# Letting four gathers go at once, and turning two engines' loops at different units of a group

## The chip, the cores and the metric

The kernel runs on one core of a Trainium2 chip. The metric is the device time of one execution in microseconds (us). Three executions of the kernel before took 2305.17, 2313.61 and 2311.89 us; the median is 2311.89. The execution that the profiler recorded took 2306.23 us.

## The reference

x is 64 sequences of 32 tokens with 512 channels. Four additions follow each other; the third is where the time goes.

```
x = x + einsum('bct,bcd->bdt', x, W0[cond])              # one of 16 mixing matrices per sequence
x = x + (x @ base.T + bias + lora(x, id))                # a linear layer with one of 32 adapters
x = x + attention(x)                                     # below
x = x + einsum('bct,bcd->bdt', x, W3[cond])

# attention, D = 128, 32 query heads, 8 key heads
q, k, v = x @ Wq.T, x @ Wk.T, x @ Wv.T                   # q and k: RMS norm, then rotary positions
kc = k_cache[block_table]                                # 16 pages of 32 positions per sequence
vc = v_cache[block_table]
scores = q @ concat(kc, k).T / sqrt(D)                   # cached positions >= seqlen are masked
o = softmax(scores) @ concat(vc, v)
out = o @ Wo.T                                           # 4096 -> 512
```

All arithmetic is fp32; many products are made as three products of rounded high parts and low remainders (high x high, high x low, low x high).

## The kernel before

Four sequences (32 tokens each) make a group of 128 rows; there are NT = 16 groups and B = 64 sequences ("batches"). After the first two layers and the projections (up to about 700 us of the trace) comes the attention. Its unit of work is one key head of one sequence with its four query heads: UG = 32 units a group, 512 in all. The instruction streams of the five engines are written by hand and meet only in semaphores. Each engine has a function `step(g, u)` with what it does in unit u of group g:

- **TensorE** computes the scores two units ahead (`score(n + 2)`, six matmuls), turns the normalised scores of this unit (`turn_p`, four transposes), makes a few matmuls of the output projection of an earlier group (`out_proj`), and the values product of the unit before (`values`, eight matmul records). At the end of each sequence come the transposes and products of the sequence's own keys (`turn_own`, and 16 small matmuls at L1290).
- **VectorE** makes the low part of the keys three units ahead (`split_k`, L999), the masked maximum two units ahead (`masked_max`, L1014), and the normalisation one unit ahead (`inverse`, `normalise`, L1020 to L1026). In some units come the low part of q (L1005, u a multiple of 4), the next mask (L991, u % 8 == 5), the low half of a finished sequence's heads (`heads_low`, L1031, after the units in `HEADS_AT`) and, in the unit `RESIDUAL`, the addition of the projected rows to the residual (L1037).
- **ScalarE** rounds keys four units ahead (`split_k`, L730), takes the exponentials one unit ahead (L744), and copies the turned scores out of PSUM (L790).
- **SyncE** loads, for each sequence, q, its own k, 16 pages of cached keys of 128 KB (L378) and its own v; it stores the heads, and loads and stores the residual rows. Its `group` function is not touched; at k == 3 it waits for `s_x2y` (the residual addition) before it stores.
- **GpSimd** gathers the cached values: four indirect DMAs of 0.5 MB a sequence (L551) by a column of row numbers each, which it first copies out of `idx_all` (L548). The gathers of sequence b go out in the four units from u = 10 + 8k on. The first waits until the products of the sequence two before are done (`s_po`), the other three each wait for TensorE's transposes of the unit before (`s_ta`).

The output projection of one group is 48 matmuls of 512 columns into one PSUM bank, `yP`. `WO_AT` says how many of them each unit of the next group holds, `WO_FROM` where they begin: from unit 4 to unit 31, one or two a unit. The first waits for the low halves of the first 16 heads and for the residual addition of the sum before (`s_x2y`), the 25th for the low halves of the others; the 24th and the last are noted (`s_woh`, `s_wo`).

Groups 1 to 14 are a hardware loop (`Fori(1, NT - 1)`) on every engine, and groups 0 and 15 are written out on either side. On TensorE (L1346), ScalarE (L821) and VectorE (L1088) the loop turns between unit 31 and unit 0, on GpSimd between units 23 and 24.

Of the kernel before, what the change touches and what calls it, by code (L numbers as in the profile page):

```python
# [36 lines left out]
BT = P // C  # L37
NT = B // BT
# [5 lines left out]
UG = BT * HK  # L44
# [6 lines left out]
H2 = HQ // 2  # L51

WO_AT = {u: 1 if u in (7, 8, 15, 16, 23, 24, 30, 31) else 2 for u in range(4, UG)}
WO_FROM, at = {}, 0
# [4 lines left out]
HEADS_AT = {2: (1, 3, 0), 5: (1, 0, 1), 6: (1, 1, 1), 8: (1, 2, 1), 10: (1, 3, 1), 18: (0, 0, 0), 21: (0, 1, 0), 26: (0, 2, 0)}  # L59
RESIDUAL = UG - 1  # L60
WO_SPLIT = 8
# [18 lines left out]
def build(nc, x, cond_row, id_row, bt_row, idx_pages, seq_tok, seq_all, w0, w3, wb, bias,  # L80
# [3 lines left out]
    with ctx:  # L84
# [133 lines left out]
        idx_all = sb("idx_all", [P, (B + 1) * 4], I32)  # L218
        idx = [sb(f"idx{i}", [P, 4], I32) for i in range(4)]
# [302 lines left out]
        def _(pool):  # L522
# [21 lines left out]
            for j in range(4):  # L544
                pool.wait_ge(s_x2st[j], 16 * (NT // 4))
            def next_idx(b, k, m):

                nc.gpsimd.tensor_copy(idx[k][:, m:m + 1], idx_all[:, bass.ds(b * 4 + m, 1)]).then_inc(s_idx, 1)  # L548

# [5 lines left out]
            pool.wait_ge(s_idx0, 1)  # L555
            for b in range(3):
                for m in range(4):
                    next_idx(b, b, m)
            pool.wait_ge(s_idx, 8)
            for m in range(4):  # L560
# [16 lines left out]
            def step(g, u):  # L577
                fixed = isinstance(g, int)
                k, m = (u - 10) // HK, (u - 10) % HK
                if m < 4 and not (fixed and not 2 <= g * BT + k + 2 < B):  # L580
                    b = g * BT + (k + 2)
                    if m == 0:
                        pool.wait_ge(s_idx, b * 4 + 4)
                        pool.wait_ge(s_po, g * BT + (k + 1))
                    else:
                        pool.wait_ge(s_ta, g * UG + u)
                    next_idx(b + 1, (k + 3) % 4, m)
                    gather_v((k + 2) % 4, k % 2, m)
# [265 lines left out]
        def _(dve):  # L854
# [190 lines left out]
            def step(g, u):  # L1045
# [13 lines left out]
                if u - 1 in HEADS_AT:  # L1059
                    back, b, half = HEADS_AT[u - 1]  # L1060
                    if not (fixed and g < back):
                        heads_low(g - back, b, half, HI_COUNT[b, half])
                if u == RESIDUAL and not (fixed and g == 0):
                    residual(g - 1)

# [15 lines left out]
            for u in range(UG):  # L1081
                if u == 4:
                    for j in range(2):
                        dve.wait_ge(s_qst[j], 16 * QKB * NT // 2)
                step(0, u)
                if 0 <= u - WO_SPLIT < H2:
                    split_wo(0, u - WO_SPLIT, wo_lo, wo_raw)
            with dve.Fori(1, NT - 1) as g:  # L1088
                for u in range(UG):
                    step(g, u)  # L1090
            for u in range(UG):
                step(NT - 1, u)
            for u in list(HEADS_AT)[:5]:
                heads_low(NT - 1, *HEADS_AT[u][1:], HI_COUNT[HEADS_AT[u][1:]])
# [36 lines left out]
        def _(pe):  # L1131
# [186 lines left out]
            def step(g, u):  # L1318
# [4 lines left out]
                turn_p(g, u)  # L1323
                if u in WO_AT and not (fixed and g == 0):
                    out_proj(g - 1, WO_FROM[u], WO_AT[u])
                if u > 0:
                    values(g, u - 1)
                elif not (fixed and n == 0):
                    values(g - 1, UG - 1)
# [14 lines left out]
            for u in range(UG):  # L1344
                step(0, u)
            with pe.Fori(1, NT - 1) as g:  # L1346
                for u in range(UG):
                    step(g, u)
            for u in range(UG):
                step(NT - 1, u)  # L1350
            values(NT - 1, UG - 1)
            out_proj(NT - 1, 0, 3 * H2)

# [78 lines left out]
```

## Time and profile before

| | |
|---|---|
| three executions | 2305.17, 2311.89, 2313.61 us |
| profiled execution | 2306.23 us |
| span from the first to the last instruction | 2304.4 us |
| busy: TensorE matmul, VectorE, ScalarE, GpSimd | 2231.9, 1754.5, 1598.8, 598.2 us |
| granted TensorE clock, mean | 0.996 of full |

A busy TensorE is not one at its peak, since its matmuls are pipelined and their ends are modelled; the time between the starts of the same operation in neighbouring units tells more. The records of an engine's sequencer (register arithmetic, branches) carry a q behind the engine's name and are not counted as busy. A loop leaves three kinds of them on its own line: one MOVE, and for each pass a FUSED_REGOPS at its beginning and a COMPARE_BRANCH at its end. An idle time in brackets stands before the instruction of its line, with what the profile takes to have ended it; "issue" is idle time in which the engine waited for nothing that the profile shows.

### The profile page before, as it was taken

How to read it: one execution, taken by the hardware profiler on the slowest of the kernel's cores; microseconds unless marked ns; L12 is line 12 of the kernel's file. 1: busy time of each engine (PE TensorE's matmuls, PEld its weight loads, DVE VectorE, ACT ScalarE, POOL GpSimd, SP SyncE). 2: the span in 40 equal slices, each digit the busy share in tenths (PEclk: the TensorE clock that was granted, in tenths of full speed). 3: DMA queues.
4: the chain of work that ended last, by engine and by line, in shares of the span. 5: the costliest groups of instructions: out<-in, count | busy, mean ns of one | idle time of the engine just before them, and what ended most of it. 6: DMA issues, size and time to landing. Idle time of an engine off the chain costs nothing.

```text
span 2304.4 us, 57131 instructions
## 1 busy us (share of the span) xinstructions
PE 2231.9 (97%) x15424; PEld 2001.3 (87%) x15424; DVE 1754.5 (76%) x5602; ACT 1598.8 (69%) x4413; POOL 598.2 (26%) x907
## 2 busy tenths in 40 slices
PE   7999999999999899999999999999999999998999
PEld 6787888888888899999999999999999999997777
DVE  3434777777778998988888888898898898995332
ACT  4423666666667988888888888888888788884221
POOL 1003444444443322222222222222222222220000
PEclk9999999999999999999999999999999999999999
DMA  5335333333337887877887877887887877864332
GB/s 170 95 114 165 102 101 102 100 101 118 101 92 251 249 255 249 260 250 249 260 252 246 258 251 244 256 257 241 256 255 246 259 254 252 256 223 179 137 123 96
DMA packets 348202, 456.58 MB, mean 198 GB/s; under 512 B 34682, under 2 KB 281018, under 8 KB 343870
## 3 DMA queue, kind: packets, MB, share of 16 engines
q1 hardware_dynamic: 308430, 315.83, 44.5%
q0 software_dynamic: 36864, 134.23, 17.4%
q10 hardware_dynamic: 2672, 4.31, 0.5%
q14 instruction: 202, 1.65, 0.3%
q8 instruction: 34, 0.56, 0.1%
HBM read 374.54 MB, written 79.69 MB: 197 GB/s over the span
## 4 chain that ended last, share of the span: by engine, by line
PE 80%; DVE 9%; issue 7%; ACT 2%; DMA 1%; ACTq 0%; DVEq 0%; SPq 0%
PE oP L1280 14%; PE S L1247 13%; PE S L1204 12%; PE oP L1204 11%; PE S L1298 8%; PE bank L1134 7%; PE bank L1311 6%; DVE k_lo L999 3%; PE oP L1134 3%; PE oP L1162 2%; DVE regC L1026 1%; PE oP L1290 1%; DVE q_lo L1005 1%; PE oP L1154 1%; PE oP L1368 1%
## 5 line engine op out<-in xcount | busy, mean ns | idle before, releaser
L1280 PEld LDWEIGHTS oP<-regC,regK 128*128 128x128 f32 x4096 | 530.8, 192 | 32.1 <-issue 1.1
L1280 PE MATMUL oP<-regC,regK 128*128 128x128 f32 x4096 | 540.8, 275 | 0.1
L730 ACT CAST k_hi<-regK 128x544 fp32r<-128x544 f32 x512 | 331.3, 647 | 130.4 <-PE S L1247 130.1
L1014 DVE CUSTOM_DVE_ANT_0 regC<-S,mask 128x544 f32<-128x544 f32 x512 | 368.9, 721 | 62.9 <-issue 56.8
L999 DVE TENSOR_TENSOR k_lo<-regK,k_hi 128x544 fp32r<-128x544 f32 x512 | 368.6, 720 | 38.1 <-ACT k_hi L730 32.6
L744 ACT ACTIVATE regC<-regC,nmx 128x544 f32<-128x544 f32 x512 | 387.2, 756 | 3.4 <-DVE nmx L1014 2.9
L548 POOL COPY idx<-idx_all 128x1 int32 (+1 forms) x260 | 65.7, 255 | 993.3 <-PE oP L1290 648.4
L1134 PE MATMUL bank<-ident,regC 128*128 128x128 f32 x2048 | 308.9, 274 | 12.7 <-DVE regC L1026 12.7
L790 ACT COPY regC<-bank 128x512 f32<-128x512 f32 x512 | 297.7, 582 | 29.2 <-PE bank L1134 29.2
L569 POOL TENSOR_TENSOR regC<-regC 128x256 f32<-128x256 f32 x320 | 245.4, 787 | 275.3 <-DVE regC L974 275.3
L551 POOL DMA_INDIRECT regK<-v_cache,idx x256 | 272.3, 1064 | 118.9 <-issue 118.1
L1247 PE MATMUL S<-k_hi,q_hi 128*128 128x288 f32 (+1 forms) x1024 | 256.3, 331 | 29.0 <-DVE nmx L1014 28.5
L1134 PEld LDWEIGHTS bank<-ident,regC 128*128 128x128 f32 x2048 | 243.5, 141 | 15.7 <-DVE regC L1026 15.5
L1026 DVE TENSOR_SCALAR regC<-regC,rinv 128x512 f32<-128x512 f32 x512 | 246.8, 482 | 0.0
L1247 PE MATMUL S<-k_hi,q_lo 128*128 128x288 f32 (+1 forms) x1024 | 214.1, 290 | 0.0
L1247 PE MATMUL S<-k_lo,q_hi 128*128 128x288 f32 (+1 forms) x1024 | 213.1, 289 | 0.0
L1247 PEld LDWEIGHTS S<-k_hi,q_hi 128*128 128x128 f32 x1024 | 155.5, 192 | 45.8 <-DVE k_lo L999 23.0
L974 DVE SCALAR_TENSOR_TENSOR regC<-oP,rstd,regK 128x128 f32<-128x128 f32 x640 | 172.8, 343 | 8.3
L974 DVE SCALAR_TENSOR_TENSOR regC<-S,rstd,regK 128x128 f32<-128x128 f32 x640 | 172.8, 344 | 8.2
L1204 PE MATMUL S<-w_hi,x2T_hi 128*128 128x512 f32 x384 | 157.6, 410 | 1.8 <-ACT regC L681 1.8
L1247 PEld LDWEIGHTS S<-k_hi,q_lo 128*128 128x128 f32 x1024 | 158.1, 190 | 0.0
L1204 PE MATMUL oP<-w_hi,x2T_hi 128*128 128x512 f32 x384 | 157.3, 410 | 0.0
(138 smaller groups left out, 4296.1 us busy)
## 6 DMA issues: line engine op xcount, KB each, us to landing
regK<-kT_cache SPq DMA_DIRECT2D x1024, 128.0 KB
qkT_d<-regC SPq DMA_DIRECT2D x160, 256.0 KB, 2.3
regC<-qkT_d SPq DMA_DIRECT2D x64, 512.0 KB, 6.7
oT_d<-regC SPq DMA_DIRECT2D x64, 256.0 KB
regK<-oT_d SPq DMA_DIRECT2D x16, 1024.0 KB, 5.2
regC<-wqk SPq DMA_DIRECT2D x10, 1024.0 KB, 5.2
v_d<-regC SPq DMA_DIRECT2D x32, 256.0 KB, 2.3
regK<-qkT_d SPq DMA_DIRECT2D x64, 128.0 KB
```

Of the source, the lines that this page charges most:

```text
L551: nc.gpsimd.indirect_dma_start(out=v_sb[par][:, m, :], out_offset=None, in_=v_cache, in_offset=bass.IndirectOffsetOnAxis(ap=idx[k][:, m:m ...
L730: nc.scalar.copy(k_hi[u % 2].rearrange("p (s t) -> p s t", t=PSIZE), k_sb[b][:, :, h, :]).then_inc(s_khi, 1)
L744: nc.scalar.activation(p, p, ACT.Exp, bias=nmx[:, u % 4:u % 4 + 1], scale=-1.0, accum_out=rs[:, u % 4:u % 4 + 1]).then_inc(s_exp, 1)
L790: nc.scalar.copy(pT_sb[u % 2], pT).then_inc(s_evA, 1)
L974: last = nc.vector.scalar_tensor_tensor(out=dst[t % 2][:, h, :], in0=bank[t % 4][:, h * D:(h + 1) * D], scalar=rstd[:, t % 4, h:h + 1], in ...
L999: nc.vector.tensor_tensor(lo, k_sb[b][:, :, h, :], hi.bitcast(F32), ALU.subtract).then_inc(s_klo, 1)
L1014: nc.vector.tensor_tensor_reduce(out=p_sb[u % 4], in0=scores, in1=mask[:], scale=-SCALE, scalar=3e38, op0=ALU.add, op1=ALU.min, accum_out= ...
L1026: nc.vector.tensor_scalar(p[:, 0:L], p[:, 0:L], rinv[:, j:j + 1], None, ALU.mult).then_inc(s_p, 1)
L1134: last = nc.tensor.transpose(dst[:, c * P:(c + 1) * P], src[:, c * P:(c + 1) * P], ident[:])
L1204: last = nc.tensor.matmul(bank[t % 4], a[:, c, rows], w[k][:, cols], start=(c == 0 and m == 0), stop=(c == HC - 1 and m == 2))
L1247: last = nc.tensor.matmul(scores[:, at], q[u // 4 % 2][:, head], k[u % 2][:, at], start=(i == 0), stop=(i == 2))
L1280: last = nc.tensor.matmul(oP[:, at:at + P], v_sb[b][:, m, h * D:(h + 1) * D], pT_sb[u % 2][:, m * P:(m + 1) * P], start=(h < 4 and m == 0) ...
```

## The change

Three things change. On GpSimd one copy takes the four columns of row numbers, and the four gathers of a sequence follow each other with no wait between them. The output projection of a group is spread over 30 units, from unit 4 of the next group to unit 1 of the one after; the residual addition moves from unit 31 to unit 2 of the group after. TensorE's loop now turns between units 1 and 2 and VectorE's between units 5 and 6; the units before are written out for group 1, and the loop's body ends with the first units of group g + 1. ScalarE and SyncE are as before.

```diff
-WO_AT = {u: 1 if u in (7, 8, 15, 16, 23, 24, 30, 31) else 2 for u in range(4, UG)}
+WO_AT = {u: 1 if u in (4, 7, 8, 11, 15, 16, 19, 23, 24, UG - 1, UG, UG + 1) else 2 for u in range(4, UG + 2)}
...
-RESIDUAL = UG - 1
+WO_TURN = 2
+RESIDUAL = 2
+TURN = 6
...
# GpSimd
-            def next_idx(b, k, m):
+            def next_idx(b, k):
 
-                nc.gpsimd.tensor_copy(idx[k][:, m:m + 1], idx_all[:, bass.ds(b * 4 + m, 1)]).then_inc(s_idx, 1)
+                nc.gpsimd.tensor_copy(idx[k][:], idx_all[:, bass.ds(b * 4, 4)]).then_inc(s_idx, 1)
...
                 if m < 4 and not (fixed and not 2 <= g * BT + k + 2 < B):
-                    b = g * BT + (k + 2)
                     if m == 0:
-                        pool.wait_ge(s_idx, b * 4 + 4)
+                        b = g * BT + (k + 2)
+                        pool.wait_ge(s_idx, b + 1)
                         pool.wait_ge(s_po, g * BT + (k + 1))
-                    else:
-                        pool.wait_ge(s_ta, g * UG + u)
-                    next_idx(b + 1, (k + 3) % 4, m)
+                        next_idx(b + 1, (k + 3) % 4)
                     gather_v((k + 2) % 4, k % 2, m)
...
# VectorE
-                if u == RESIDUAL and not (fixed and g == 0):
-                    residual(g - 1)
+                if u == RESIDUAL and not (fixed and g < 2):
+                    residual(g - 2)
...
+            for u in range(TURN):
+                step(1, u)
             with dve.Fori(1, NT - 1) as g:
-                for u in range(UG):
+                for u in range(TURN, UG):
                     step(g, u)
-            for u in range(UG):
+                for u in range(TURN):
+                    step(g + 1, u)
+            for u in range(TURN, UG):
                 step(NT - 1, u)
+            residual(NT - 2)
...
# TensorE
-                if u in WO_AT and not (fixed and g == 0):
+                if u in WO_AT and not (fixed and g < 1):
                     out_proj(g - 1, WO_FROM[u], WO_AT[u])
+                if u < WO_TURN and not (fixed and g < 2):
+                    out_proj(g - 2, WO_FROM[UG + u], WO_AT[UG + u])
...
+            for u in range(WO_TURN):
+                step(1, u)
             with pe.Fori(1, NT - 1) as g:
-                for u in range(UG):
+                for u in range(WO_TURN, UG):
                     step(g, u)
-            for u in range(UG):
+                for u in range(WO_TURN):
+                    step(g + 1, u)
+            for u in range(WO_TURN, UG):
                 step(NT - 1, u)
             values(NT - 1, UG - 1)
+            out_proj(NT - 2, WO_FROM[UG], 3 * H2 - WO_FROM[UG])
             out_proj(NT - 1, 0, 3 * H2)
```

## Rows read from the trace of the kernel before

**Rows 1.** The page: instruction fetches (packets, MB, share), and the chain by engine.

```profile
q14 instruction: 202, 1.65, 0.3%
...
PE 80%; DVE 9%; issue 7%; ACT 2%; DMA 1%; ACTq 0%; DVEq 0%; SPq 0%
```

**Rows 2.** TensorE's attention loop line: count, ns min/median/max, first and last start.

```profile
L1346 PEldq FUSED_REGOPS  x14: 50/50/55, 811.3 to 1921.6; - x14
...
L1346 PEldq COMPARE_BRANCH  x14: 76/208/208, 893.9 to 2006.3; - x14
```

**Rows 3.** TensorE's timeline, a group's start: start, us, what, idle before.

```profile
1240.64 0.49 PE L1247 MATMUL S<-k_hi,q_hi 128*128 128x288 f32 x2 [1.08 <-DVE nmx L1014]
...
1242.41 0.66 PE L1134 MATMUL bank<-ident,regC 128*128 128x128 f32 x4 [0.78 <-DVE regC L1026]
```

**Rows 4.** VectorE's timeline, the same start.

```profile
1236.18 0.69 DVE L1037 TENSOR_TENSOR regC<-bank,regC 128x512 f32<-128x512 f32 x1
1239.12 0.72 DVE L999 TENSOR_TENSOR k_lo<-regK,k_hi 128x544 fp32r<-128x544 f32 x1 [2.25 <-ACT k_hi L730]
...
1241.72 0.24 DVE L1025 TENSOR_SCALAR regC<-regC,rinv 128x32 f32<-128x32 f32 x1 [1.15 <-issue]
```

**Rows 5.** One jump of the attention loops: VectorE's line L1088, ScalarE's L821.

```profile
L1088 DVEq COMPARE_BRANCH  x1: 56/56/56, 1235.8 to 1235.8; - x1
L1088 DVEq FUSED_REGOPS  x1: 63/63/63, 1239.0 to 1239.0; - x1
...
L821 ACTq COMPARE_BRANCH  x1: 45/45/45, 1235.4 to 1235.4; - x1
L821 ACTq FUSED_REGOPS  x1: 41/41/41, 1235.6 to 1235.6; - x1
```

**Rows 6.** One jump of VectorE's projection loop.

```profile
L1067 DVEq COMPARE_BRANCH  x1: 63/63/63, 463.5 to 463.5; - x1
L1067 DVEq FUSED_REGOPS  x1: 85/85/85, 466.3 to 466.3; - x1
```

**Rows 7.** Waits of 900 to 1930 us: in total, times, longest.

```profile
DVE regC L1025 <- issue: 16.6, 12, 2.0
```

**Rows 8.** TensorE's timeline, transposes of three units; from 1249.38 with two projection matmuls.

```profile
1247.29 0.60 PE L1134 MATMUL bank<-ident,regC 128*128 128x128 f32 x4
...
1249.38 0.60 PE L1134 MATMUL bank<-ident,regC 128*128 128x128 f32 x4
...
1251.92 0.60 PE L1134 MATMUL bank<-ident,regC 128*128 128x128 f32 x4
```

**Rows 9.** VectorE's timeline, units without a stall.

```profile
1231.40 0.48 DVE L991 TENSOR_SCALAR mask<-iota,seqf 128x512 f32<-128x512 f32 x1
...
1242.27 0.68 DVE L1005 TENSOR_TENSOR q_lo<-regC,q_hi 128x512 fp32r<-128x512 f32 x1
...
1244.90 0.72 DVE L999 TENSOR_TENSOR k_lo<-regK,k_hi 128x544 fp32r<-128x544 f32 x1
...
1246.93 0.72 DVE L999 TENSOR_TENSOR k_lo<-regK,k_hi 128x544 fp32r<-128x544 f32 x1
...
1248.96 0.42 DVE L1031 TENSOR_TENSOR oT_lo<-regC,oT_hi 128x256 fp32r<-128x256 f32 x1
```

**Rows 10.** GpSimd's timeline: first and last held gather of a batch, one not held.

```profile
1262.89 0.96 POOL L551 DMA_INDIRECT regK<-v_cache,idx  x1 [0.38 <-issue]
...
1271.84 1.07 POOL L551 DMA_INDIRECT regK<-v_cache,idx  x1 [0.50 <-issue]
...
726.17 0.94 POOL L551 DMA_INDIRECT regK<-v_cache,idx  x1 [0.30 <-issue]
```

**Rows 11.** SyncE's timeline: the 16 page loads of one batch.

```profile
1255.99 8.41 SPq L378 DMA_DIRECT2D regK<-kT_cache  x16
```

**Rows 12.** One stretch: us, busy us of each engine, clock, DMA share, GB/s.

```profile
727.00:730.00 3.00, 2.92 (x13) 2.55 (x13) 2.96 (x9) 2.08 (x6) 1.53 (x2) 0.50 1.03 342
```

**Rows 13.** ScalarE's waits, 900 to 1930 us.

```profile
ACT k_hi L730 <- PE S L1247: 103.2, 228, 0.8
```

More of the change, by code:

```diff
@@ L555, in _ @@
             pool.wait_ge(s_idx0, 1)
[L556 to L559, printed above, removed]
+            next_idx(0, 0)
+            next_idx(1, 1)
+            next_idx(2, 2)
+            pool.wait_ge(s_idx, 2)
             for m in range(4):
```

## The prediction

> **What bounds the kernel now.** I read the page first, then the loop lines, then the timelines around one jump. In the page the reader is to see that TensorE carries the chain that ended last (80%), that VectorE has 9% and "issue" 7% [rows 1]. The attention stretch is where this chain can give: TensorE is busy back to back there, except at one place in each group. The loop line of TensorE shows it: the first pass of its loop runs from 811.3 to the branch at 893.9, 82.6 us, and the 13 further passes up to the last branch at 2006.3 take 1112.4 us, 85.57 us each [rows 2]. The first pass is entered without a jump, the other 13 begin with one. So a jump costs 85.57 - 82.6 = 3.0 us, 13 x 3.0 = 39 us in all. That is the only stall worth speaking of in this stretch, and the change moves what stands around it.
>
> Who stalls is seen around 1240: TensorE waits 1.08 us for VectorE's maximum and 0.78 us for its normalised scores [rows 3]. VectorE itself has two holes, 2.25 us behind the residual addition and 1.15 us two operations later [rows 4]. The first is put down to ScalarE's k_hi, but the loop line tells another story: VectorE's branch is at 1235.8 and the first instruction behind it at 1239.0, 3.2 us later, whereas ScalarE's comes 0.2 us after its branch [rows 5] and TensorE's branch takes 0.208 us in all [rows 2]. VectorE's projection loop shows the same: branch 463.5, next 466.3 [rows 6]. The second hole recurs: 12 times, 16.6 us in sum [rows 7].
>
> **Why one loop jumps free and the other doesn't.** The code is fetched in pieces: 202 packets for 1.65 MB, 8.2 KB each [rows 1]. In the compiled program of the kernel before every instruction is 64 bytes, so a piece holds 128. Counted in it, the attention loops of ScalarE and VectorE have 261 and 309 instructions, VectorE's projection loop 403. A loop of 261 lies in three pieces, one of 403 in four at least. If four pieces are held and the fourth is the one fetched ahead, a loop in three finds its start still there, a loop in four does not. VectorE's 309 can be either. The second hole says which: it comes some 9 instructions behind the loop's start [rows 4], as if a piece ended there and the next was asked for only then. 9 + 128 + 128 + 44 is four pieces, so it must fetch. This is my inference, not a row.
>
> The Trainium skill (Runtime: NRT & Kernel Launch, Instruction fetch mechanics) says that a taken branch whose target is outside a window of two pages has to wait for a fetch; it gives pages of 256 instructions. By pages of 256 the projection loop of 403 would fit in two at its place, and the row shows it paying 2.8 us, so I go by the pieces of 128 that the packets show.
>
> **The change part by part.**
>
> *VectorE's loop at unit 6.* Six units of group 1 are now written out ahead of the loop. VectorE issues seven instructions a unit, and in units 0 to 5 two splits of q, one low half and a mask more: 46 (the residual is left out in group 1). The loop's start moves 46 behind its old place: 128 + 9 - 46 = 91 instructions are left of its first piece. 91 + 128 + about 100 is three pieces. The body may grow by some register instructions for group g + 1; there is room for 38. So I expect VectorE's jump to become as short as ScalarE's, 0.2 us under work in flight, and both holes to go: -39 us, less what is late next. The bounds: nothing goes (rival A), or all 39.
>
> *What is late next.* TensorE's own branch (0.208 us [rows 2], of which some 0.15 us is lost) stays: 13 x 0.15 = 2 us. It is part of the 85.57 and moves to unit 2, where no other engine jumps. Then units 0 to 5: TensorE goes 2.09 us a unit without the projection and 2.54 with two of its matmuls, 0.23 each [rows 8]. VectorE goes 2.03 us a unit [rows 9], and its extras are a split of q (0.68) twice, a low half (0.42), a mask (0.48), and now the residual (0.69) [rows 4, 9], each about 0.08 less net, since neighbours overlap. TensorE over units 0 to 5: 6 x 2.09, five projection matmuls of 0.23 and the 16 small ones of the own values, which I estimate at three such matmuls, 0.7: 14.4 us. VectorE: 6 x 2.03 + 1.2 + 0.34 + 0.4 + 0.6 = 14.7 us. VectorE comes out 0.3 us behind, of which its lead hides a part; the bounds are 0 and 0.7, I take 0.4 us a group, 13 x 0.4 = 5 us.
>
> *The projection on into units 0 and 1.* 48 matmuls before and after; only their places change. Two of them fill TensorE's lightest units. The end of the sum is noted at unit 1, the residual waits for it at unit 2 of VectorE's order, and the next sum begins at unit 4 behind it: two units, about 4 us, of room. SyncE's store of the residual waits for the same and has the next group's q, own k and 16 pages behind it; it reaches that wait about when unit 2 ends, and its loads of own k wait for unit 4 anyway: 0 us, at most 1 us a group if it comes late. The turning point of the high halves (unit 18) comes one unit closer, 0. After the last group two matmuls of group 14 fall into the time in which TensorE waits for the last low halves: 0.
>
> *Index copies.* Four copies of 1 column become one of 4: GpSimd idles there, 0.
>
> *Gathers not held.* In the trace the four of a batch go out at 1262.89 to 1271.84, nine us apart; where nothing holds them each takes 0.94 us and 0.30 us lie between, so one goes every 1.25 us [rows 10]. What they meet is the pages of keys: SyncE issues 16 of a batch from 1255.99 to 1264.4 [rows 11], the last two or three just as the first gather of 0.5 MB starts. Four at once are 2.1 MB; at the 342 GB/s, share 1.03, that the engines moved when four were out together [rows 12] they fill over 6 us in which the last pages get a part only. The gathers are freed in unit 8 of a pair of batches and ScalarE's split wants the keys in unit 12: three and a half units of some 2.5 us, 8.7 us. Bounds: 0 if the last pages still land first; if they land with the last gather, about 10.5 us after, ScalarE is late by 1.8 us, less the 0.45 us it idles a unit anyway (103.2 us in 228 waits [rows 13]), 1.2 us a batch over 62 batches = 74 us. Only two or three pages are exposed and a share of the engines is theirs, so I take a value near the lower end, 0.05 us a batch, 3 us. A gain from earlier values: no row shows TensorE waiting for them, 0.
>
> The Trainium skill (DMA: Bandwidth & Descriptors, Queues, rings and completion order) says that each DMA engine goes round robin between its queues by packets. By that the last pages, 0.4 MB at half of 342 GB/s, would take 2.3 us instead of 1.2: a batch with under 1 us of room would be late, the others not; this speaks for a price but a small one.
>
> **The sum.** Against the profiled execution (2306.2 us; span 2304.4): -39 + 2 + 5 + 3 = -29, so 2277. The three runs of before have their median 5.7 us above the profiled one, and reach from 2305 to 2314; I put the median of after at 2278.
>
> **Rivals.**
> A. VectorE's loop still needs a fetch (the body is longer than I count, or pieces are held otherwise). Then 3.2 us between branch and next instruction stand at unit 6, with only the normalisation and the mask to run meanwhile, about 0.8 us. The hole is 2.4 us, and VectorE has no lead left after units 0 to 5, so TensorE loses nearly all: 2.4 + 0.3 of the units against 3.0 now. Saved 0.3 x 13 = 4 us; with the gathers' 3 us the time is 2305 to 2311, no change. With a second hole of 1.15 us, 15 us more: 2320. For it: VectorE pays in both of its long loops [rows 5, 6]. Against: ScalarE doesn't, and the place of the second hole.
> B. The keys come late: the gathers take the DMA engines while pages are still due. It decides from 0.5 us a batch: 62 x 0.5 = 31 us eats the jump's gain. At 0.8 us of late keys per batch, 50 us, it is 2277 - 3 + 50 = 2324. For it: with four gathers out the DMA engines have nothing left [rows 12]. Against: only two or three of 16 pages are still due then, and ScalarE has idle time [rows 13].
> C. The jump is free, but half of the gain is spent by VectorE in units 0 to 5 or by late keys in one batch of four (1.2 us x 15): 2290.
>
> **How the numbers follow.** Forecast 0.55, C 0.15, A 0.18, B 0.12. Predicted 2278. The range takes in C and the most of A: 2264 (nothing late next, the full 39 and the small 3 us not paid) to 2311. A measurement here can tell 0.5%, 11.6 us: under 2300 is faster, over 2323 slower. Faster: forecast and C and a little of A, 0.71. Same: A and half of B, 0.20. Slower: 0.09.
>
> **What would show it.** Right: VectorE's branch followed within 0.3 us, no wait of TensorE for its maximum at a group's start, passes of the TensorE loop of about 83 us, fewer than 202 instruction packets. The gathers 1.25 us apart, and no wait of ScalarE's k_hi for a DMA. Wrong: a hole of over 2 us at VectorE's unit 6 (A), or waits for pages of keys (B).

## The result, and the profile after

The changed kernel takes 2368.18 us, the median of its four executions, against 2312.75: 1.0234 of the time before, with a 95% interval of 1.0208 to 1.0261. The forecast was 2278 us. The profiled execution took 2367.95 us. (One of the four took 3580.5 us at a granted clock of 0.58; the ratio leaves it out, and the other three lie between 2366.5 and 2368.4 us.)

The page of the changed kernel: its span, the instruction fetches and the chain by engine as in [rows 1], and the chain by line.

```profile
span 2366.2 us, 56604 instructions
...
q14 instruction: 137, 1.12, 0.1%
...
PE 73%; issue 8%; SPq 8%; DMA 6%; DVE 3%; ACT 2%; ACTq 0%; DVEq 0%
PE oP L1285 12%; PE S L1209 11%; PE oP L1209 11%; PE S L1252 10%; PE S L1303 8%; PE bank L1139 7%; PE bank L1316 5%; SPq L380 4%; DMA regK<-kT_cache 4%; PE oP L1139 3%; SPq L378 2%; PE oP L1167 2%; PE oP L1295 1%; DVE k_lo L999 1%; ACT regC L790 1%
```

Two things are to be seen. The instruction packets fell from 202 to 137, and VectorE's share of the chain from 9% to 3%: what the change was expected to do, it did. And the chain has new members, SyncE's sequencer with 8% and the page loads with 6%, where there were none and 1%.

The loop lines, as in [rows 2] and [rows 5]: TensorE's (all passes), then VectorE's and SyncE's around one jump.

```profile
L1355 PEldq FUSED_REGOPS  x14: 50/50/55, 817.8 to 1983.5; - x14
...
L1355 PEldq COMPARE_BRANCH  x14: 76/208/208, 906.6 to 2073.8; - x14
```

```profile
L1090 DVEq COMPARE_BRANCH  x1: 56/56/56, 1273.9 to 1273.9; - x1
L1090 DVEq FUSED_REGOPS  x1: 63/63/63, 1274.2 to 1274.2; - x1
```

```profile
L470 SPq COMPARE_BRANCH  x1: 45/45/45, 1267.8 to 1267.8; - x1
L470 SPq FUSED_REGOPS  x1: 41/41/41, 1273.2 to 1273.2; - x1
```

A pass of TensorE's loop now takes (2073.8 - 906.6) / 13 = 89.8 us, not the 83 expected nor the 85.57 of [rows 2]. VectorE's branch is followed after 0.3 us (3.2 before). SyncE's is followed after 5.4 us; between 1000 and 1900 us this was 5.0 to 6.3 us in every group, and 2.7 to 3.7 in the kernel before. I had never looked at SyncE's jump. In the kernel before the same jump, in the same place of its pass, is this one:

```profile
L468 SPq COMPARE_BRANCH  x1: 45/45/45, 1245.1 to 1245.1; - x1
L468 SPq FUSED_REGOPS  x1: 41/41/41, 1248.5 to 1248.5; - x1
```

What follows from it, in the order of time. First SyncE's timeline (start, us, what), then GpSimd's of the same stretch (brackets: idle before, and what ended it).

```profile
1265.53 0.38 SPq L458 DMA_DIRECT2D oT_d<-regC  x1
1267.25 0.37 SPq L467 DMA_DIRECT2D x_d<-regC  x1
1273.55 0.36 SPq L389 DMA_DIRECT2D regC<-qkT_d  x1
1274.18 0.35 SPq L385 DMA_DIRECT2D regK<-qkT_d  x1
1280.00 9.11 SPq L380 DMA_DIRECT2D regK<-kT_cache  x16
```

```profile
1282.14 0.55 POOL L550 COPY idx<-idx_all 128x4 int32 x1 [14.71 <-PE oP L1295]
1282.84 0.96 POOL L553 DMA_INDIRECT regK<-v_cache,idx  x1 [0.16 <-issue]
...
1286.83 1.09 POOL L553 DMA_INDIRECT regK<-v_cache,idx  x1 [0.30 <-issue]
```

SyncE stores the heads, then waits until 1267.2 for the residual addition, stores it, jumps (5.4 us), asks for q and own k, reads 16 page numbers (5.8 us from own k to the first page), and issues 16 pages until 1289.1. The four gathers go out from 1282.84 to 1287.9. The first starts when only five of the 16 pages have been issued, so eleven come behind it. Before, the first gather started as the last two or three pages were issued [rows 10, 11]. Now the same operations on ScalarE, then on TensorE, and a table of stretches (us, busy us of each engine, clock, DMA share, GB/s):

```profile
1290.24 0.19 ACT L744 ACTIVATION_READ_ACCUMULATOR regC<-regC,nmx 128x1 f32 x1
1296.49 0.64 ACT L730 CAST k_hi<-regK 128x544 fp32r<-128x544 f32 x1 [6.07 <-DMA regK<-kT_cache]
1297.04 0.58 ACT L790 COPY regC<-bank 128x512 f32<-128x512 f32 x1
```

```profile
1290.14 0.60 PE L1139 MATMUL bank<-ident,regC 128*128 128x128 f32 x4
...
1297.77 1.09 PE L1139 MATMUL bank<-ident,regC 128*128 128x128 f32 x4 [4.91 <-ACT regC L790]
...
1302.57 0.99 PE L1139 MATMUL bank<-ident,regC 128*128 128x128 f32 x4
...
1305.51 0.61 PE L1139 MATMUL bank<-ident,regC 128*128 128x128 f32 x4
```

```profile
1290.00:1293.00 3.00, 2.86 (x23) 2.55 (x21) 2.45 (x8) 0.43 (x2) 0.00 (x0) 1.00 1.03 396
1293.00:1297.50 4.50, 0.00 (x0) 0.00 (x0) 0.33 (x1) 1.01 (x2) 0.00 (x0) 0.89 0.93 335
1297.50:1300.00 2.50, 2.23 (x9) 2.07 (x10) 2.46 (x9) 2.50 (x6) 0.00 (x0) 0.50 0.16 42
1300.00:1304.00 4.00, 4.00 (x21) 3.91 (x21) 1.37 (x7) 1.26 (x4) 0.00 (x0) 0.58 0.81 247
1304.00:1308.00 4.00, 4.00 (x36) 3.96 (x35) 3.13 (x10) 3.08 (x8) 0.00 (x0) 1.00 0.76 231
```

ScalarE waits 6.07 us for a page, with the copy of the turned scores behind it in its order. TensorE needs that copy and stands still for 4.91 us. Then comes a second price: the granted clock falls to 0.50, the level of 1.2 GHz, and stays there for some 5 us. The same four transposes take 1.09 and 0.99 us and not 0.60. The unit from 1297.77 to 1302.57 takes 4.80 us and the next 2.94, where units at the full clock take 2.3 to 2.6. This is one of the longer cases: the clock fell behind each of the 14 holes of this kind, and behind them 28 us of full-speed time were not granted in all, 2.0 us a hole. The Trainium skill (TensorE: Matmul & The Clock Gate, Part 1) says that TensorE's clock is halved when the engine has had too little to do, and given back once it is busy again; these rows agree, at 0.50 and 1.00.

It happens once a group. The waits between 900 and 1930 us (us in all, times, longest):

```profile
ACT k_hi L730 <- PE S L1252: 97.6, 170, 2.6
ACT k_hi L730 <- DMA regK<-kT_cache: 70.6, 12, 7.0
...
PE bank L1139 <- ACT regC L790: 56.8, 12, 5.9
```

The row of [rows 13] is about as it was. The row on `kT_cache` is new; no engine waited for a page in this stretch before. It is always the sequence whose pages SyncE issues right behind its jump, one of the four in a group.

### The profile page after: what moved, and what is told of

Same layout as the page of the kernel before. It is cut to its first block, busy times and chain, and to the rows that moved or that the text cites. A ratio compares the mean times of both kernels' runs of the same rounds, so it can differ in the third digit from the quotient of the medians.

```text
span 2366.2 us, 56604 instructions
## 1 busy us (share of the span) xinstructions
PE 2257.1 (95%) x15424; PEld 2027.6 (86%) x15424; DVE 1756.6 (74%) x5602; ACT 1597.1 (67%) x4413; POOL 555.4 (23%) x712
## 4 chain that ended last, share of the span: by engine, by line
PE 73%; issue 8%; SPq 8%; DMA 6%; DVE 3%; ACT 2%; ACTq 0%; DVEq 0%
PE oP L1285 12%; PE S L1209 11%; PE oP L1209 11%; PE S L1252 10%; PE S L1303 8%; PE bank L1139 7%; PE bank L1316 5%; SPq L380 4%; DMA regK<-kT_cache 4%; PE oP L1139 3%; SPq L378 2%; PE oP L1167 2%; PE oP L1295 1%; DVE k_lo L999 1%; ACT regC L790 1%
## 5 line engine op out<-in xcount | busy, mean ns | idle before, releaser
L1285 PEld LDWEIGHTS oP<-regC,regK 128*128 128x128 f32 x4096 | 542.9, 195 | 33.8 <-issue 1.1
L1285 PE MATMUL oP<-regC,regK 128*128 128x128 f32 x4096 | 551.9, 279 | 0.1
L1139 PE MATMUL bank<-ident,regC 128*128 128x128 f32 x2048 | 313.9, 277 | 66.0 <-ACT regC L790 66.0
L550 POOL COPY idx<-idx_all 128x4 int32 (+1 forms) x65 | 28.3, 437 | 1128.2 <-PE oP L1295 1030.3
L553 POOL DMA_INDIRECT regK<-v_cache,idx x256 | 266.8, 1042 | 80.7 <-issue 80.4
L1252 PEld LDWEIGHTS S<-k_lo,q_hi 128*128 128x128 f32 x1024 | 160.1, 192 | 0.0
```

The costliest lines, as they stand in the source:

```text
L553: nc.gpsimd.indirect_dma_start(out=v_sb[par][:, m, :], out_offset=None, in_=v_cache, in_offset=bass.IndirectOffsetOnAxis(ap=idx[k][:, m:m ...
L1139: last = nc.tensor.transpose(dst[:, c * P:(c + 1) * P], src[:, c * P:(c + 1) * P], ident[:])
L1252: last = nc.tensor.matmul(scores[:, at], q[u // 4 % 2][:, head], k[u % 2][:, at], start=(i == 0), stop=(i == 2))
L1285: last = nc.tensor.matmul(oP[:, at:at + P], v_sb[b][:, m, h * D:(h + 1) * D], pT_sb[u % 2][:, m * P:(m + 1) * P], start=(h < 4 and m == 0) ...
```

## The experiments

Differences between kernels are given below as differences of their ratios times 2313 us, so that each is measured against the kernel before on its own chip.

**The gathers held as before (e1_held), and the change's GpSimd part alone (e2_unheld_only).**

```diff
 # e1_held: the changed kernel, with GpSimd's program of before
+                    else:
+                        pool.wait_ge(s_ta, g * UG + u)
+                    next_idx(b + 1, (k + 3) % 4, m)
 # e2_unheld_only: the kernel before, with these waits gone and one copy of four columns
```

> The changed kernel with GpSimd as before: single index copies, gathers two to four held. In the trace of the changed kernel SyncE's loop jump takes 5.4 us (3.4 before), since its fetch falls among four gathers; the last page of the one late sequence in each group is issued 4.7 us later than before and lands 7.6 us after its issue (6.1 before), and ScalarE waits up to 7 us for it, 14 times. Theory 1 (SyncE comes late for three reasons: VectorE's stall no longer covers it, 3.0 us; its fetch is 2.0 us longer; it waits 1.3 us for the residual): only the fetch and the sharing of the engines are mended, the wait falls from 6 us to 1 to 3 us a group, the time to 2285 to 2310. Theory 2 (the gathers alone delay the pages): the wait goes, 2270 to 2280. Theory 3 (the gathers don't matter, all is lost cover): 2350 to 2368.

> The kernel before with the changed GpSimd alone: one index copy, four gathers in a row; loops and projection as before. Theory 1: VectorE's stall of 3 us at the group's start still covers SyncE, the fetch of SyncE's jump grows from 3.4 to over 5 us, the late sequence had 0.3 to 1 us of room, so ScalarE waits 1 to 3 us a group beyond its idle time: 2325 to 2350. Theory 2: the pages are late as in the changed kernel, 6 us a group, about 2390. Theory 3: no change, 2306 to 2315.

Measured: e1_held 2305.05 us, 0.9962 [0.9947, 0.9977]; e2_unheld_only 2337.37 us, 1.0120 [1.0079, 1.0162]. Held gathers don't bring the 39 us either. Of e1_held, SyncE's loop line around one jump, ScalarE's waits for pages (900 to 1930 us), and TensorE behind one such wait:

```profile
L470 SPq COMPARE_BRANCH  x1: 45/45/45, 1245.7 to 1245.7; - x1
L470 SPq FUSED_REGOPS  x1: 41/41/41, 1250.7 to 1250.7; - x1
```

```profile
ACT k_hi L732 <- DMA regK<-kT_cache: 37.9, 11, 4.1
```

```profile
1187.64 0.63 PE L1141 MATMUL bank<-ident,regC 128*128 128x128 f32 x4 [2.80 <-ACT regC L792]
```

The keys are late there too, 3.4 us each time instead of 5.9; after a hole of 2.80 us the four transposes take 0.63 us, so the clock has stayed up. In e2_unheld_only, where nothing is turned, they are late in six groups of twelve:

```profile
ACT k_hi L728 <- DMA regK<-kT_cache: 16.3, 6, 5.3
```

So there are two causes, neither small: the gathers, and something in the rest of the change. Both end in the same wait.

**VectorE's loop alone (e3_turn_only), and no loop turned but the code shifted (e4_pad46).** e4_pad46 is the kernel before with 46 writes of one column at the head of VectorE's program; nothing reads them.

```diff
 # e3_turn_only: the kernel before; residual, projection and GpSimd as before
+            for u in range(6):
+                step(1, u)
             with dve.Fori(1, NT - 1) as g:
-                for u in range(UG):
+                for u in range(6, UG):
                     step(g, u)
-            for u in range(UG):
+                for u in range(6):
+                    step(g + 1, u)
+            for u in range(6, UG):
                 step(NT - 1, u)
 # e4_pad46: the kernel before
+            for i in range(46):
+                nc.vector.memset(padt[:, i:i + 1], 0.0)
```

> The kernel before with VectorE's loop alone turned at unit 6 (six units of group 1 written out; residual addition still at unit 31, gathers held, projection and TensorE's loop as before). The loop starts 46 instructions later. If the fetch pieces decide: both holes of VectorE go, 39 us of jumps. Theory 1: of this something comes back, since the pages of one sequence a group had 0.3 to 1 us of room and lose 3 us of cover: ScalarE waits 0.5 to 2 us a group, 2275 to 2300. Theory 2: nothing comes back, 2268 to 2275. If pieces don't decide and the jump is paid at unit 6 as well: about 2306.

> The kernel before with 46 one-column memsets of an unused tile at the head of VectorE's program, where it waits for the first loads anyway; nothing else. Only the place of the code is moved: the attention loop of VectorE then lies in three pieces of 128 instructions, not four. If the pieces decide: the branch is followed within 0.3 us, both holes go though the loop still turns between units 31 and 0, and the time is that of turning the loop at unit 6 alone, 2270 to 2300. If it is the place of the turn in the group that matters: no change, 2306 to 2315, with the branch at 3 us.

Measured: e3_turn_only 2275.46 us, 0.9830 [0.9796, 0.9864]; e4_pad46 2272.70 us, 0.9825 [0.9796, 0.9854]. The page of e4_pad46, its chain, and VectorE's loop line around one jump:

```profile
q14 instruction: 137, 1.12, 0.2%
...
PE 92%; DVE 2%; issue 2%; DMA 2%; SPq 1%; ACT 1%; POOLq 0%; POOL 0%; ACTq 0%; DVEq 0%
```

```profile
L1091 DVEq COMPARE_BRANCH  x1: 56/56/56, 1228.1 to 1228.1; - x1
L1091 DVEq FUSED_REGOPS  x1: 63/63/63, 1228.4 to 1228.4; - x1
```

46 instructions that do nothing bring 40 us. The place of the loop in the code is the whole cause of the old stall, as the prediction had it; where the loop turns is not. A little comes back as late pages: ScalarE waits for pages 6 times in e3_turn_only, 6.2 us in all, and 4 times in e4_pad46, 4.8 us in all, 3.8 us the longest (900 to 1930 us).

**The store of the residual moved (e5_store_later, e6_held_later).** SyncE's wait for `s_x2y` and its store go from the end of its pass, ahead of the jump, behind the first sequence of the next pass. (SyncE's pass of group 1 is written out for it, so its loop jumps once less.) e6_held_later also has GpSimd's program of before.

```diff
+                    if k == 0 and store:
+                        sp.wait_ge(s_x2y, g - 1)
+                        sp.dma_start(x2_d[...g - 2...], x2r).then_inc(s_x2yst, 16)
...
-                    if k == 3 and not first:
+                    if k == 3 and last:
                         sp.wait_ge(s_x2y, g)
```

> The changed kernel with SyncE's store of the residual rows moved from the end of its own pass (k == 3) to k == 0 of the next pass, behind that sequence's pages and own v; group 1 of SyncE is written out for it, so its loop turns 13 times. Nothing else. In the changed kernel SyncE waits 1.3 us for the residual at this store just ahead of its jump, and the last page of the late sequence goes out 7.1 us after the products of the sequence two before; with the gathers held it is 5.8 (2.1 in the kernel before, 3.6 where VectorE's jump alone is free). Theory 1 (all of SyncE's late time counts): the 1.3 us go, and the 0.6 us of the store with them; ScalarE's wait of some 6 us falls to about 4, 13 groups: 2335 to 2350. Theory 2 (the gathers' share of the engines alone): no change, 2362 to 2370.

> The changed kernel with both: gathers held as before, and the store of the residual rows moved behind the next sequence's pages. Left of the change: VectorE's free jump, the residual at unit 2, the projection over 30 units, TensorE's turn at unit 2. Theory 1: the last page goes out 3.6 us after as where VectorE's jump alone is free, and next to no wait is left; the group takes 82.0 to 82.9 us: 2258 to 2278. If the new places of the projection and the residual cost something of themselves, it stays at 2290 or above.

Measured: e5_store_later (gathers as changed) 2345.74 us, 1.0136 [1.0114, 1.0158]; e6_held_later (gathers held) 2273.31 us, 0.9816 [0.9798, 0.9834]. ScalarE's wait for pages is gone from e6_held_later between 900 and 1930 us, and its TensorE loop takes (1978.5 - 899.6) / 13 = 83.0 us a pass:

```profile
L1361 PEldq COMPARE_BRANCH  x14: 83/215/215, 899.6 to 1978.5; - x14
```

With held gathers the wait for the residual cost 0.9962 - 0.9816 = 0.0146, 34 us; with the gathers as changed, 1.0234 - 1.0136 = 0.0098, 23 us. It is 1.3 us a group by itself (1265.9 to 1267.2 above), but it also delays the jump into a stretch where its fetch takes longer: 4.8 to 5.4 us in e1_held, 2.7 to 3.2 in e6_held_later. The packet records of the trace say why. In e6_held_later SyncE's branch is at 1235.0, its packet of 8 KB starts on a DMA engine at 1236.1, and SyncE goes on at 1237.8; in e1_held these are 1245.7, 1249.1, 1250.7; in the changed kernel 1267.8, 1271.6, 1273.2. The packet itself takes 0.3 us in the last two. What differs is how long after the branch it starts. From the branch to that start, packets of gathered values fill a share of 0.74 of the 16 DMA engines in the changed kernel, 0.63 in e1_held and 0.11 in e6_held_later. That the fetch stands behind them in a queue is the likely reading; the trace doesn't show the order in the queue.

**The stall put back at the new place (e7_turn_pad50).** e3_turn_only with 50 writes of one column at the head of VectorE's program, so that its loop lies in four pieces again.

```diff
+            for i in range(50):
+                nc.vector.memset(padt[:, i:i + 1], 0.0)
```

> VectorE's loop turned at unit 6 in the kernel before (2275 us), with 50 one-column memsets of an unused tile at the head of VectorE's program. The loop's start moves from 91 to 41 instructions ahead of a piece's end, and its 311 instructions lie in four pieces again. If the pieces decide: the jump is paid, at unit 6, 2.4 us of a hole and no second one, instruction packets back from 137 to about 200, time 2295 to 2315. If turning at unit 6 is what helped: 2270 to 2280 as without the memsets.

Measured: 2342.47 us, 1.0110 [1.0087, 1.0132]. The page, VectorE's loop line around one jump, TensorE's timeline behind it, and a stretch after that:

```profile
q14 instruction: 202, 1.65, 0.2%
```

```profile
L1093 DVEq COMPARE_BRANCH  x1: 63/63/63, 1174.7 to 1174.7; - x1
L1093 DVEq FUSED_REGOPS  x1: 63/63/63, 1179.1 to 1179.1; - x1
```

```profile
1180.74 0.79 PE L1254 MATMUL S<-k_hi,q_hi 128*128 128x288 f32 x2 [3.26 <-DVE nmx L1017]
```

```profile
1183.00:1186.00 3.00, 3.00 (x15) 2.90 (x14) 1.89 (x7) 1.34 (x4) 0.00 (x0) 0.50 0.84 247
```

The packets are back to 202 and the stall is back, which fits the count of pieces from the other side. Three places of the loop have now been seen: by that count 9 and 41 instructions ahead of a piece's end it pays, 91 ahead it is free. That pieces of 128 are held in fours remains an inference which these three fit. The stall costs more than it did: (2044.9 - 894.7) / 13 = 88.5 us a pass, 5.5 above the 83.0 of a kernel without stalls, where at the old place it cost 3.0; the expectation had this wrong. Before, the stall reached TensorE as two short holes of 1.08 and 0.78 us [rows 3] at a clock of 1.00. Here it is one of 3.26 us, and the clock falls to 0.50 behind it. The jump also takes 4.4 us, not 3.2. Over the waits of 900 to 1930 us TensorE's hole is 3.7 us in the mean (44.7 us in 12). Some 1.7 us a pass are full-speed time not granted (21.4 us over the 13 passes). Together that is nearly the 5.5.

**The page numbers read earlier, gathers held (e8_held_later_numbers).** SyncE reads the 16 numbers before it waits for the low keys, not behind own k.

```diff
                         load_q(b, k % 2)
+                        pages = numbers(btab[0:1, k * NPP:(k + 1) * NPP])
                         sp.wait_ge(s_klo, g * UG + HK * (k + 1))
                         load_own_k(b, k % 2)
-                        load_pages(btab[0:1, k * NPP:(k + 1) * NPP], k % 2)
+                        load_numbered(pages, k % 2)
```

> As the run with gathers held and the store moved, and SyncE reads the 16 page numbers of a sequence into registers (5.4 us between own k and the first page in the trace) before it waits for VectorE's low keys, not behind. Theory 1: pages go out 1 to 3 us earlier for every sequence, no wait for pages is left at all, the spread between executions shrinks: 2255 to 2270. If the page loads were not what is late: no difference to the run without it.

Measured: 2273.19 us, 0.9815 [0.9796, 0.9833], the same as e6_held_later. Once the keys come in time, earlier is worth nothing.

**The free jump and the changed gathers, nothing else (e9_pad46_unheld).** The kernel before with e4_pad46's 46 writes and the changed GpSimd program.

```diff
+            for i in range(46):
+                nc.vector.memset(padt[:, i:i + 1], 0.0)
...
-                    else:
-                        pool.wait_ge(s_ta, g * UG + u)
-                    next_idx(b + 1, (k + 3) % 4, m)
+                        next_idx(b + 1, (k + 3) % 4)
```

> The fourth corner of a square: the kernel before with the 46 memsets (VectorE's jump free) and the changed GpSimd (one index copy, gathers in a row), residual, store and projection as before. The other three: neither 2313, gathers alone 2337, free jump alone 2273. Theory 1 (the two share the late sequence's little room, so their costs add up to more than their sum): ScalarE's wait is 3 to 5 us a group, 2315 to 2345, above the 2297 that adding the two effects gives. Theory 2 (independent effects): 2290 to 2300.

Measured: 2363.80 us, 1.0217 [1.0190, 1.0244]; 91 us above e4_pad46, while the same edit costs 28 us without the free jump. That is above even the range of theory 1: the wait is 5.7 us a group, not 3 to 5, and the clock, which the expectation left out, falls as well. Its waits (900 to 1930 us):

```profile
ACT k_hi L729 <- DMA regK<-kT_cache: 68.2, 12, 6.1
...
PE bank L1135 <- ACT regC L789: 51.5, 12, 4.7
```

Here TensorE's projection, the residual addition and its store are as before, and the loss is all there. The price of the gathers depends on the stall that the other part removes: in e2_unheld_only the keys are late in 6 of 12 groups, here in all 12, and TensorE's holes are longer (4.3 us each), which costs clock: its mean is 0.986, and 0.997 in e4_pad46.

**SyncE without a loop (e10_sync_written_out).** The changed kernel, SyncE's passes of groups 1 to 14 written out one behind the other.

```diff
-            with sp.Fori(1, NT - 1) as g:
+            for g in range(1, NT - 1):
                 group(g, False, False)
```

> The changed kernel with SyncE's 16 groups written out, so that SyncE never jumps in the attention; gathers in a row, wait for the residual and all else as changed. In the changed kernel the jump takes 5.4 us and the last page goes out 7.1 us after the products of the sequence two before. Theory 1 (SyncE's time counts): without the 5.4 us the last page goes out at about 2 us, ScalarE's wait of some 6 us falls to 0 to 3, time 2275 to 2310. Theory 2 (sharing of the DMA engines counts): the last page still lands over 8 us after its issue, 2335 to 2365.

Measured: 2279.70 us, 0.9853 [0.9827, 0.9878]. The page:

```profile
q14 instruction: 108, 0.88, 0.1%
...
PE 89%; DVE 4%; issue 3%; ACT 2%; DMA 2%; SPq 1%; ACTq 0%; DVEq 0%
```

All three edits of the change are in it, the unheld gathers too, and no wait for a page is left between 900 and 1930 us. So the loss needs SyncE's jump: without it, and with the same gathers, the kernel is only 9 us above e6_held_later (0.9853 - 0.9816). The two also differ in the place of the store.

**The page numbers earlier, gathers as changed (e11_later_numbers).** e5_store_later with the edit of e8.

```diff
+                        pages = numbers(btab[0:1, k * NPP:(k + 1) * NPP])
                         sp.wait_ge(s_klo, g * UG + HK * (k + 1))
```

> The changed kernel with gathers in a row, store of the residual moved behind the next sequence's pages, and the page numbers read before the wait for the low keys. Without the last item it takes 2346, the last page goes out at 5.1 us and lands at 13.4, wanted at 8.4. With the gathers held the same item moved the last page from 2.4 to 1.5 us, and the other sequences' by 2 to 4 us. Theory 1: pages about 1 us earlier in the late sequence, 13 us in all: 2325 to 2340.

Measured: 2275.55 us, 0.9837 [0.9810, 0.9864]: 69 us below e5_store_later, far below what I expected. Not every page is in time: ScalarE still waits for pages 5 times, 4.9 us in all and 1.6 us at most (900 to 1930 us). I had reckoned that behind the jump the numbers take the same 5.4 us whether read before or behind own k, and that is so (q at 1240.01, first page 6.4 us later; in e5_store_later 1261.70 and also 6.4):

```profile
1234.03 0.39 SPq L472 DMA_DIRECT2D oT_d<-regC  x1
1240.01 0.35 SPq L399 DMA_DIRECT2D regC<-qkT_d  x1
1245.91 0.34 SPq L395 DMA_DIRECT2D regK<-qkT_d  x1
1246.43 8.43 SPq L390 DMA_DIRECT2D regK<-kT_cache  x16
```

What I missed is the sequence ahead of the jump. There SyncE waits for the low keys anyway and reads its numbers meanwhile, its last page goes out 4.2 us earlier, and the jump starts 1.7 us earlier. The table shows it in time.

**Both cures without the change (e12_pad46_numbers).** e4_pad46 with the edit of e8: gathers held, loops and projection as in the kernel before.

```diff
+            for i in range(46):
+                nc.vector.memset(padt[:, i:i + 1], 0.0)
...
+                        pages = numbers(btab[0:1, k * NPP:(k + 1) * NPP])
                         sp.wait_ge(s_klo, g * UG + HK * (k + 1))
```

> The kernel before with the 46 memsets (2273) and the page numbers read before the wait for the low keys. In the run with the memsets four waits for pages were left, 4.8 us between 900 and 1930 us, in one group 2.6 us. Expected: these go, 2268 to 2273; a chance of the best time of all. If the numbers matter nowhere: 2273 again.

Measured: 2271.29 us, 0.9815 [0.9790, 0.9841], the lowest median of all, and under both kernels. It can't be told from e4, e6 and e8 (2272.7, 2273.3, 2273.2). Of the four waits for pages of e4_pad46 one of 0.4 us is left, so 4.4 us of ScalarE's waits were worth next to nothing. (The longest of the four was 3.8 us on ScalarE and 2.4 us on TensorE, not the 2.6 of the expectation.)

**One table of them all.** Read from the traces: SyncE's branch, its q, its last page, that page landed, and ScalarE's first use, for the sequence behind the jump; in us from the end of the small products (L1290) of the sequence two before, which is where the gathers start; medians over the 13 such sequences from group 2 on.

| | branch | q | last page | landed | used |
|---|---|---|---|---|---|
| before | -16.9 | -13.4 | 2.1 | 7.8 | 8.7 |
| e4_pad46 | -14.7 | -10.9 | 3.6 | 8.4 | 8.7 |
| e2_unheld_only | -17.7 | -11.7 | 2.9 | 9.2 | 9.3 |
| e9_pad46_unheld | -14.8 | -8.4 | 6.7 | 14.1 | 14.2 |
| changed kernel | -14.2 | -8.4 | 7.1 | 14.3 | 14.4 |
| e5_store_later | -15.5 | -9.5 | 5.1 | 13.4 | 13.5 |
| e1_held | -14.2 | -8.9 | 5.8 | 11.7 | 11.8 |
| e6_held_later | -15.5 | -12.3 | 2.4 | 7.3 | 8.4 |
| e11_later_numbers | -17.2 | -12.1 | 2.4 | 7.9 | 8.4 |
| e10_sync_written_out | none | -13.0 | 2.2 | 6.9 | 8.4 |

The keys are wanted at 8.4 to 8.7. The kernel before has 0.8 us of room, e4_pad46 0.3. These are medians; single sequences land up to some 4 us later (12.2 in one group of e4_pad46). Where the last page is issued by 2.4, the median lands in time, unheld gathers or not (5.5 us later in e11_later_numbers, where 5 of the 13 land 0.5 to 1.6 us after the keys are wanted). Where it is issued from 5.1 on, with the gathers unheld, it takes 7.2 to 8.3 us to land: the gathers are then ahead of it, and the DMA engines are full (396 GB/s at a share of 1.03 from 1290 to 1293 us, above).

## Why the prediction was wrong

*VectorE's stall ends with four pieces becoming three.* Right, in mechanism and size: -39 us forecast, -39 and -40 us in e3_turn_only and e4_pad46, and a jump paid again in e7_turn_pad50. Its signs were there: 0.3 us behind the branch, 137 packets, TensorE's passes of 83 us wherever the keys are in time. TensorE's waits for the maximum don't vanish, between 900 and 1930 us they shrink from 19.1 us in 24 waits to 3.7 us in 12, 0.3 us each.

*What is late next.* I took 0.4 us a group for units 0 to 5 and 2 us in all for TensorE's own branch. A group without any jump takes 82.6 us [rows 2], e6_held_later 83.0: right. But "what is late next" was asked of VectorE and TensorE alone. The engine that was late next was SyncE.

*SyncE's wait for the residual, "0 us, at most 1 us a group".* Wrong: 34 us, 2.4 a group. I wrote that its loads of own k wait for the low keys anyway. In the kernel before they do, for about 0.7 us (q at 1248.86, own k at 1250.18); in the changed kernel own k follows q at once (1273.55, 1274.18), so nothing hides the lost time. In [rows 11] the pages start at 1255.99, and the numbers they need take over 5 us to read; I took the issue of 16 pages as the whole of SyncE's work, and left out its jump, its reading of numbers, and that all of them stand in one order behind the wait.

*Gathers not held, 3 us, and the reason that only two or three pages are exposed.* This is the step that failed, and the largest: 63 us between e1_held and the changed kernel, 91 us between e4_pad46 and e9_pad46_unheld. The overlap of pages and gathers was read from a trace in which VectorE's stall of 3 us (1235.8 to 1239.0) held TensorE and the gathers back while SyncE went on issuing pages, 9 us ahead of its own jump (1245.1 to 1248.5). That gave SyncE its room. In the table, taking that stall away moves the branch from -16.9 to -14.7 and eats 0.6 of the 0.8 us of room. The four gathers then add to SyncE's jump (3.8 us from branch to q in e4_pad46, 6.4 in e9_pad46_unheld), the last page goes out 3 us later, and it lands 7.4 us behind its issue, not 4.8. Rival B had this in kind, with 0.8 us of late keys in each of 62 sequences, 2324 us and a chance of 0.12. It is 5.9 us in one sequence of four, and it has a second term that no rival of mine had, the clock.

*The account.* From e6_held_later, which is the changed kernel without late keys, to the changed kernel it is 1.0234 - 0.9816, 97 us. Over the whole run TensorE waits 66.0 us for the copy behind the late keys (15 times). The mean clock is 0.984 over 2366.2 us against 0.995 over 2271.8: 37.9 against 11.4 us of full-speed time not granted, 26.5 us more. Some 3 us of these fall into the waits themselves, where they cost nothing more. Together it is some 90 us, of the 94.4 between the two profiled spans. How much of the late landing is page packets behind gather packets, and how much only the later issue, was not measured apart; e11_later_numbers shows that issue in time is enough.

*Rival A,* the stall moved but not gone, was priced at no change. e7_turn_pad50 is this case with the gathers held, at 1.0110. The price failed twice: TensorE's hole was put at 2.4 us and is 3.7 in the mean, since the jump takes 4.2 to 6.2 us there and not 3.2, and the clock costs some 1.7 us a pass more.

*Two slips in its sums,* which change nothing above. The upper bound for late keys is 1.8 - 0.45 = 1.35 us a batch, 84 us and not 74. The lower end of the range, nothing late next and the 3 us not paid, is 2277 - 10 = 2267 us and not 2264.

## What to carry to other kernels

Before a stall is taken out, ask of every engine, the one that only issues transfers above all, what it does during that stall: how far its last transfer lands ahead of its use (here 0.8 us), and what stands in its order ahead of it (a loop's jump, reading numbers, a wait for somebody's sum). Two edits that draw on the same room don't add: -40 and +28 us gave +50. If a hardware loop jumps slowly, a few idle instructions ahead of it can be the whole cure (e4_pad46, -40 us), and reading page numbers ahead of a wait took nearly all of the late pages away (e11_later_numbers, -69 us against e5_store_later).

## What the runs showed of the hardware that I had not expected

- A loop's jump that needs a fetch is a transfer like others, and it takes longer when data is moving. SyncE's packet itself takes 0.3 us in the changed kernel; from the branch to its start pass 3.9 us there and 1.2 us in e6_held_later. The whole jump takes 5.0 to 7.0 us with the gathers unheld (e2_unheld_only, the changed kernel), 2.7 to 3.7 us in the kernel before. Held gathers alone don't keep it short: in e1_held, where it starts later, it is 4.8 to 5.4 us.
- A hole of TensorE can have a second price. All 11 holes of 1.6 to 2.9 us in e1_held left the clock at 1.00. All 14 of 3.8 to 5.9 us in the changed kernel were followed by 0.50, for 2.9 to 5.9 us, which is 2.0 us of full-speed time each. The length of the hole alone does not decide: in e5_store_later one of 3.4 us left the clock up and one of 2.8 us was followed by 0.50, and in the kernel before it fell once in the loop, at 1328.6, behind one of 1.7 us.
- The same loop of VectorE (310 records a pass in the trace) is free or costs 5 us a pass, by where the first of its instructions lies. e3_turn_only and e7_turn_pad50 differ only by 50 idle instructions ahead, and by 0.028 in their ratios, 65 us.
